# An eighth table read by one-hot products, one eviction per pick, and transposes issued a group ahead in a DLRM tower

## The chip, the cores and the metric

The kernel runs on one core of a Trainium2 chip. The metric is the device time of the core in microseconds (us), lower is better. A core has a matrix engine (TensorE, PE in the rows, its weight loads PEld), a vector engine (VectorE, DVE), a scalar engine (ScalarE, ACT), GpSimd (POOL) and SyncE (SP), which here only issues DMAs. Each engine runs its own instructions in order; between engines there are only semaphores.

## What is computed

For 512 samples, 26 rows of 128 numbers are looked up in 26 tables. All pairwise dot products of the 27 vectors of a sample (its dense vector and the 26 rows) go with the dense vector into a three-layer perceptron.

```python
e = jnp.stack([tbl_0[ids[:, 0]], ..., tbl_25[ids[:, 25]]], axis=1)      # 512 x 26 x 128
sd = jnp.einsum('bfd,bd->bf', e, dense)                                 # 26 dots
ss = jnp.einsum('bfd,bgd->bfg', e, e); pairs = ss[:, iu, ju]            # 325 dots
h = jnp.concatenate([dense, sd, pairs, dense], axis=1)                  # 512 x 607
h = jnp.maximum(h @ W_top1 + b_top1, 0.0)                               # 512
h = jnp.maximum(h @ W_top2 + b_top2, 0.0)                               # 256
y = h @ W_top3                                                          # 512 x 1
```

Eleven tables have 1250 rows, six 1000, the others 12500 and more.

## The kernel before

The batch is cut into four tiles of 128 samples, t = 0 to 3. The semaphore waits and the order of every engine's work are written out by hand.

**Hot tables, the pick stage.** Seven tables (`HOT`) are not gathered. Each is loaded whole, as 125 partitions of 8 rows (1000 rows) or 10 rows (1250 rows); one row per partition is a step. For table i, `spread_ids(i)` copies the 512 ids to all partitions with two matmuls (L342). ACT makes the rounded high part of the table (`round_table`, L757) and DVE the low part (`low_part`, L612). For each step a one-hot matrix of 512 columns says which sample wants the row: DVE makes most of them, two steps in an instruction (`one_hots`, L602), ACT makes the steps of `KS_ACT` in two instructions each (`distances`, L766, and L775). `pick(i)` sums high and low products of all steps in PSUM (L351), two 512-column matmuls a step. ACT reads the result out in two instructions (`read_picked`, L730 and L732): the first two tiles (`DIRECT = 2`) go straight into `vecs`, where the dot products are taken from, the other two into `early`, from which `place_early(2)` and `place_early(3)` (L746) bring them to `vecs` later. The one-hots lie in a ring of `HOT_STEPS` = 24 steps, the high and low parts in rings of 20.

**Cold tables.** The other 19 are joined in one tensor, and GpSimd gathers 128 rows with an indirect DMA (L323), 19 for each tile, 76 in all. They come in seven groups g = 0 to 6 a tile; `transposes(t, g)` turns a group on PE (L387, one 128-column matmul for each gather), `read_transposed(t, g)` copies it to `vecs` (DVE L590 for even g, ACT L737 for odd g). The rows of tiles 2 and 3 are gathered into the buffers of tiles 0 and 1, after their transposes.

**Dots and layers.** `gram(t, part)` takes the dots of 32 samples (L410, 8 matmuls; the trace counts 16). The last part of a tile is cut in two pieces, of the last tile in three. DVE and ACT copy them out (`read_sums`, L648 and L800). When the last part's sums are out, SP moves the tile's dots to the partitions that layer 1 wants with nine DMAs (`move_strips`, L275), and `layer_1(t)` (L438) waits for all of them (`s_dots[t]`). `layer_1_dense(t)` (L423) adds the dense part first. `layer_2(t)` and `layer_3(t)` follow. The last part of tile 3 is moved with matmuls (`move_last_part`, L451) and its other parts by five DMAs of SP and four of GpSimd (L333).

Of the kernel before, what the change touches and what calls it, by code (L numbers as in the profile page):

```python
# [11 lines left out]
P = 128  # L12
# [4 lines left out]
PITCH = 32  # L17
# [6 lines left out]
HOT = [5, 6, 7, 16, 19, 24, 2]  # L24
# [8 lines left out]
KS_ACT = [[4, 5, 6] if i in (1, 2, NHOT - 1) else [4, 5] for i in range(NHOT)]  # L33
# [6 lines left out]
HOT_STEPS, PART_STEPS, TABLE_RING = 24, 20, 3  # L40
EARLY = 1 + NHOT

DIRECT = 2
# [9 lines left out]
EXTRA_WIDTHS = [w for w in (1, 2, 4) if (len(COLD) - MAIN) & w]  # L53
assert EXTRA_WIDTHS[0] == 1
# [29 lines left out]
def build(nc, ins, out):  # L84
    with ExitStack() as ctx:
# [14 lines left out]
        dense_t = sb("dense_t", [P, TILES, P])  # L100
        early = sb("early", [P, EARLY, (TILES - DIRECT) * P])
# [48 lines left out]
        s_table = [sem(f"s_table{i}") for i in range(NHOT)]  # L150
        s_w1_dense = sem("s_w1_dense")
# [16 lines left out]
        s_picked = sem("s_picked")  # L168
        s_pick_read = sem("s_pick_read")
# [56 lines left out]
        def by_sample(x):  # L226


            return x.rearrange("d (h g s) -> d h s g", s=QUADS, g=PER_PART)
# [31 lines left out]
        def _(sp):  # L261
            def load_table(i):
# [3 lines left out]
                sp.dma_start(table[0:KP_A, i % TABLE_RING, 0:KTS[i]], whole[0:KP_A]).then_inc(s_table[i], 16)  # L266
# [37 lines left out]
        def _(pool):  # L304
            nc.gpsimd.memset(ident[:, :], 0.0).then_inc(s_zero, 1)
# [30 lines left out]
        def _(pe):  # L336
# [53 lines left out]
            def gram(t, part, piece=None):  # L390
                if part == 0:

                    if t < DIRECT:
                        pe.wait_ge(s_pick_read, NHOT)
                    else:
                        pe.wait_ge(s_early, t - DIRECT + 1)
                    pe.wait_ge(s_dve_read, uses_to(t, 0))
# [17 lines left out]
            def layer_1_dense(t):  # L415
# [5 lines left out]
                for bank, o0 in ((ps_h_act, OC1 // 2), (ps_h_dve, 0)):  # L421
                    for o in range(OC1 // 2):
                        pe.matmul(bank[:, o, :], w1_fold[:, (o0 + o) * P:(o0 + o + 1) * P], dense_t[:, t, :],  # L423
                                  start=(o == 0), stop=False, skip_group_check=True)
# [70 lines left out]
            pick(0)  # L495
            pick(1)
            transposes(0, 0)
            pick(2)
            transposes(0, 1)
            pick(3)  # L500
            transposes(0, 2)
            pick(4)
            transposes(0, 3)
            pick(5)
            transposes(0, 4)
            transposes(0, 5)
            pick(6)
            transposes(0, 6)
            transposes(1, 0)
            pe.wait_ge(s_pad, 2)  # L510
            pe.wait_ge(s_dense_read, 2)

            gram(0, 0)
            transposes(1, 1)
            gram(0, 1)
            transposes(1, 2)
            gram(0, 2)
            gram(0, 3, 0)
            gram(0, 3, 1)
            transposes(1, 3)  # L520
            gram(1, 0)
            transposes(1, 4)
            gram(1, 1)
            transposes(1, 5)
            transposes(1, 6)
            gram(1, 2)
            gram(1, 3, 0)
            gram(1, 3, 1)
            layer_1_dense(0)
            transposes(2, 0)  # L530
            layer_1(0)
            transposes(2, 1)
# [3 lines left out]
            transposes(2, 2)  # L536
            layer_1_dense(1)
            gram(2, 1)
            transposes(2, 3)
            transposes(2, 4)  # L540
            gram(2, 2)
            transposes(2, 5)
            gram(2, 3, 0)
            transposes(2, 6)
            gram(2, 3, 1)
            layer_1(1)
            transposes(3, 0)
            layer_2(1)
            layer_3(1)
            transposes(3, 1)  # L550
            layer_1_dense(2)
            gram(3, 0)
            layer_1(2)
            transposes(3, 2)
            layer_2(2)
            gram(3, 1)
            layer_3(2)
            transposes(3, 3)
            gram(3, 2)
# [14 lines left out]
        def _(dve):  # L574
# [40 lines left out]
            for i in range(NHOT):  # L615
# [5 lines left out]
                if i == 2:  # L621
                    dve.wait_ge(s_dense_tp, 1)
                    nc.vector.tensor_copy(dense_t[:, :, :], ps_dve[:, :, :]).then_inc(s_dense_read, 1)
                if i == 3:
                    read_transposed(0, 0)
                if i == 5:
# [285 lines left out]
```

## Time and profile before

| what | value |
|---|---|
| median of 3 runs | 119.66 us (117.87 to 120.6) |
| the profiled execution | 118.84 us |
| its span, first to last instruction | 116.9 us |
| PE busy | 104.5 us (89%) |
| POOL busy | 75.7 us (65%) |
| DVE busy | 63.5 us (54%) |
| ACT busy | 58.5 us (50%) |

The span lies 1.94 us below the execution's own time. Busy shares are averages over two stages: up to about 47 us the seven picks, with PE, DVE and ACT all full, and after it the dots and layers, with PE full and the other two half idle.

### The profile page before, as it was taken

To read this page: it belongs to the slowest core of one execution; us is meant where nothing else is said; L and a number is where in the kernel's file an instruction comes from. 1 tells how busy PE (TensorE), PEld (TensorE's weight loads), DVE (VectorE), ACT (ScalarE), POOL (GpSimd) and SP (SyncE) were. 2 spreads that over 40 slices of the span, in tenths; PEclk is the share of its full clock that TensorE was granted. 3 is DMA by queue.
4 is the path that set the end of the run, shared out by engine and by line. 5 is a ranking of instruction groups with operands and counts; after the bars stand their busy time and mean duration, and the time that the engine had idled before them with its cause. 6 is when DMAs were issued, how large, how long until landed. Compare 5 with 4: busy or idle time off the path is not lost.

```text
span 116.9 us, 1946 instructions
## 1 busy us (share of the span) xinstructions
PE 104.5 (89%) x696; PEld 90.7 (78%) x696; DVE 63.5 (54%) x140; ACT 58.5 (50%) x133; POOL 75.7 (65%) x88
## 2 busy tenths in 40 slices
PE   0679999999999688999999999978989997899991
PEld 0366676686868475999998998877979996799981
DVE  4779959997999990356746135225220343350030
ACT  4299549939976991255477235535212414340200
POOL 3777777677677767767767767767777775070000
PEclk9999999999999999999999999999999999999599
DMA  2997617362869822212233233112223112011000
GB/s 45 276 275 188 208 52 227 70 203 72 247 201 258 317 83 53 59 45 60 61 72 93 70 78 88 51 45 65 61 68 101 48 45 67 6 25 25 0 0 1
DMA packets 5709, 11.71 MB, mean 100 GB/s; under 512 B 2600, under 2 KB 3070, under 8 KB 5701
## 3 DMA queue, kind: packets, MB, share of 16 engines
q1 hardware_dynamic: 3141, 6.55, 18.9%
q0 software_dynamic: 2560, 5.05, 17.0%
q8 instruction: 5, 0.08, 0.3%
q14 instruction: 3, 0.02, 0.1%
HBM read 10.86 MB, written 0.00 MB: 93 GB/s over the span
## 4 chain that ended last, share of the span: by engine, by line
PE 79%; SPq 6%; DMA 5%; issue 3%; DVE 2%; ACT 2%
PE ps_gram L351 27%; PE ps_gram L410 19%; PE ps_h_bank L438 11%; SPq L275 5%; DMA dense<-in_r_dense_features 4%; PE ps_dve L387 3%; PE ps_h_bank L466 3%; PE ps_h_bank L423 3%; PE ps_act L387 3%; PE ps_gram L342 2%; DMA dots<-sums_even 2%; PE ps_dve L451 2%; PE ps_h_bank L478 1%; PE ps_h_bank L342 1%; PE ps_h_bank L469 1%
## 5 line engine op out<-in xcount | busy, mean ns | idle before, releaser
L323 POOL DMA_INDIRECT rows<-in_cold,cold_rows x72 | 68.8, 955 | 21.9 <-issue 21.3
L410 PE MATMUL ps_gram<-vecs 128*122 128x108 f32 x256 | 30.3, 271 | 2.3 <-ACT vecs L737 1.4
L410 PEld LDWEIGHTS ps_gram<-vecs 128*122 128x122 f32 x256 | 28.6, 187 | 3.5 <-ACT vecs L737 2.5
L351 PE MATMUL ps_gram<-one_hot,table_hi 125*128 125x512 f32 x58 | 24.7, 447 | 1.3 <-issue 1.3
L602 DVE TENSOR_TENSOR one_hot<-ps_gram,row_id 125x1024 fp32r<-125x1024 f32 (+1 forms) x22 | 25.0, 1138 | 0.7 <-PE ps_h_bank L342 0.7
L351 PE MATMUL ps_gram<-one_hot,table_lo 125*128 125x512 f32 x58 | 23.5, 426 | 0.0
L351 PEld LDWEIGHTS ps_gram<-one_hot,table_hi 125*128 125x128 f32 x58 | 11.7, 210 | 5.8 <-issue 3.0
L351 PEld LDWEIGHTS ps_gram<-one_hot,table_lo 125*128 125x128 f32 x58 | 12.0, 207 | 2.7
L438 PE MATMUL ps_h_bank<-dots,w_dots 128*128 128x128 f32 x96 | 13.2, 301 | 0.2 <-DMA dots<-sums_even 0.2
L612 DVE TENSOR_TENSOR table_lo<-table,table_hi 125x256 fp32r<-125x256 f32 x29 | 11.7, 412 | 2.9 <-ACT table_hi L757 2.8
L438 PEld LDWEIGHTS ps_h_bank<-dots,w_dots 128*128 128x128 f32 x96 | 12.7, 215 | 0.4 <-issue 0.4
L648 DVE COPY sums_even<-ps_gram 26x216 f32<-26x216 f32 (+1 forms) x20 | 6.5, 327 | 10.9 <-PE ps_gram L410 10.7
L590 DVE COPY vecs<-ps_dve 128x128 f32<-128x128 f32 (+2 forms) x20 | 8.1, 436 | 7.8 <-PE ps_dve L387 7.7
L800 ACT COPY sums_even<-ps_gram 26x216 f32<-26x216 f32 (+1 forms) x20 | 5.9, 296 | 11.1 <-PE ps_gram L410 10.9
L648 DVE COPY table<-ps_gram 26x216 f32<-26x216 f32 (+2 forms) x22 | 6.8, 310 | 7.6 <-PE ps_gram L410 7.2
L800 ACT COPY table<-ps_gram 26x216 f32<-26x216 f32 (+2 forms) x22 | 6.2, 283 | 9.1 <-PE ps_gram L410 8.9
L766 ACT ACTIVATE distance<-ps_h_bank,minus_row_id 125x512 f32<-125x512 f32 x17 | 10.6, 690 | 0.0
L757 ACT CAST table_hi<-table 125x1024 fp32r<-125x1024 f32 (+2 forms) x8 | 7.6, 966 | 5.1 <-PE ps_gram L351 2.9
L775 ACT ACTIVATE one_hot<-distance 125x512 fp32r<-125x512 f32 x17 | 9.7, 640 | 0.0
L737 ACT COPY vecs<-ps_act 128x512 f32<-128x512 f32 (+1 forms) x12 | 5.8, 480 | 6.2 <-PE ps_act L387 6.1
L656 DVE TENSOR_SCALAR h<-ps_h_bank,b 128x128 f32<-128x128 f32 x8 | 2.4, 346 | 11.5 <-PE ps_h_bank L438 11.5
L387 PE MATMUL ps_dve<-ident,rows 128*128 128x128 f32 x40 | 7.0, 274 | 0.5 <-DVE vecs L590 0.5
(63 smaller groups left out, 96.2 us busy)
## 6 DMA issues: line engine op xcount, KB each, us to landing
table<-in_tbl SPq DMA_DIRECT2D x6, 448.0 KB
rows<-in_cold,cold_rows POOLq DMA_INDIRECT x72, 2.5
w_dots<-in_w_dots SPq DMA_DIRECT2D x1, 768.0 KB, 5.6
table<-in_tbl SPq DMA_DIRECT2D x1, 560.0 KB
w_dense<-in_w_dense SPq DMA_DIRECT2D x1, 512.0 KB, 3.7
w<-in_W_top SPq DMA_DIRECT2D x1, 512.0 KB, 8.2
table<-in_tbl SPq DMA_DIRECT2D x6, 52.0 KB
dense<-in_r_dense_features SPq DMA_DIRECT2D x1, 256.0 KB, 4.2
```

Source lines behind the costliest of these rows:

```text
L323: pool.indirect_dma_start(out=rows[:, t % ROW_SETS, n, :], out_offset=None, in_=ins["cold"], in_offset=bass.IndirectOffsetOnAxis(ap=(cold_ ...
L351: return pe.matmul(ps_pick[:, i % 2, :], part[0:KP, (STEP_AT[i] + k) % PART_STEPS, :], one_hot[0:KP, (STEP_AT[i] + k) % HOT_STEPS, :], sta ...
L387: last = pe.transpose(bank[:, n - n0, :], rows[:, t % ROW_SETS, n, :], ident[:, :])
L410: last = pe.matmul(ps_gram[0:TAKEN, b0 + (g - g0) // PER_BANK, c0:c0 + COLS], vecs[:, t % 2, p0:p0 + QUADS, :].rearrange("d p f -> d (p f) ...
L438: last = pe.matmul(bank[:, o, :], w1_dots[:, j, (o0 + o) * P:(o0 + o + 1) * P], dots[:, t, :, j, :], start=False, stop=(j == STEPS - 1), s ...
L590: last = nc.vector.tensor_copy(dst, src)
L602: nc.vector.tensor_tensor(one_hot[0:KP, m:m + k1 - k0, :], ps_ids_dve[0:KP, i % 2, :].unsqueeze(1).to_broadcast(shape), row_id[0:KP, at + ...
L612: nc.vector.tensor_sub(table_lo[0:KP, n:n + PIECE], table[0:KP, i % TABLE_RING, k:k + PIECE], table_hi[0:KP, n:n + PIECE].bitcast(F32)).th ...
L648: last = nc.vector.tensor_copy(*own_sums(t, part, s, piece))
L766: nc.scalar.activation(distance[0:KP, n, :], ps_ids_act[0:KP, i % 2, :], ACT.Abs, bias=minus_row_id[0:KP, at + k:at + k + 1]).then_inc(s_d ...
L775: nc.scalar.activation(one_hot[0:KP, (STEP_AT[i] + k) % HOT_STEPS, :], distance[0:KP, n, :], ACT.Relu, bias=1.0, scale=-1.0).then_inc(s_ho ...
L800: last = nc.scalar.copy(*own_sums(t, part, s, piece))
```

## The change

- An eighth table (3, with 1250 rows) is picked, and the order of the tables is new. The steps go from 58 to 68, the gathers from 76 to 72 (18 a tile), `KS_ACT` gives ACT three steps of every table but tables 0 and 4, and the ring of one-hots has 22 steps.
- `read_picked` is one copy of 512 columns into `early`. `DIRECT` is gone, and the picked rows and the dense row of every tile are placed in `vecs` by copies from `early`: of tile 0 by ACT (parts 0 and 2) and DVE (parts 1 and 3), of tiles 1 to 3 by `place_early` on ACT. `dense_t` is now `early[:, 0]`.
- The larger piece of table 0's load (112 partitions) is issued by GpSimd, ahead of everything else there.
- On PE, picks 0 to 6 stand in a row with no transposes between them; most transposes stand one group further ahead of the gram that needs them, and the layers of a tile stand elsewhere among the grams.

```diff
-HOT = [5, 6, 7, 16, 19, 24, 2]
+HOT = [5, 6, 2, 7, 16, 3, 19, 24]
-KS_ACT = [[4, 5, 6] if i in (1, 2, NHOT - 1) else [4, 5] for i in range(NHOT)]
+KS_ACT = [[4, 5] if i in (0, 4) else [4, 5, 6] for i in range(NHOT)]
-HOT_STEPS, PART_STEPS, TABLE_RING = 24, 20, 3
+HOT_STEPS, PART_STEPS, TABLE_RING = 22, 20, 3
-DIRECT = 2
...
+        def placing(t, part):
+            p0 = part * PITCH
+            return (vecs[:, t % 2, p0:p0 + PITCH, 0:EARLY].rearrange("d (g s) f -> d f s g", s=QUADS),
+                    early[:, :, t * P + p0:t * P + p0 + PITCH].rearrange("d f (s g) -> d f s g", s=QUADS))
...
+            pool.dma_start(table[0:KP_A, 0, 0:KTS[0]], ins[f"tbl_{HOT[0]}"].rearrange("(p k) d -> p k d", k=KTS[0])[0:KP_A]
+                           ).then_inc(s_table_0_pool, 16)
...
             def gram(t, part, piece=None):
+                if t == 0:
+                    pe.wait_ge(s_placed_dve if part % 2 else s_placed_act, part // 2 + 1)
+                elif part == 0:
+                    pe.wait_ge(s_early, t)
...
             def read_picked(i):
                 act.wait_ge(s_picked, i + 1)
-                nc.scalar.copy(by_sample(vecs[:, :, :, 1 + i].rearrange("d t p -> d (t p)")),
-                               ps_pick[:, i % 2, 0:DIRECT * P].rearrange("d (h s g) -> d h s g", s=QUADS, g=PER_PART))
-                nc.scalar.copy(early[:, 1 + i, :], ps_pick[:, i % 2, DIRECT * P:]).then_inc(s_pick_read, 1)
+                nc.scalar.copy(early[:, 1 + i, :], ps_pick[:, i % 2, :]).then_inc(s_pick_read, 1)
...
# ACT, behind the picks
             read_picked(NHOT - 1)
+            act.wait_ge(s_dense_read, 1)
+            act.wait_ge(s_pick_read, NHOT)
+            nc.scalar.copy(*placing(0, 0)).then_inc(s_placed_act, 1)
+            read_transposed(0, 3)
+            nc.scalar.copy(*placing(0, 2)).then_inc(s_placed_act, 1)
...
# PE, tile 2's last grams and what follows
-            gram(2, 3, 1)
-            layer_1(1)
+            layer_2(1)
+            gram(2, 3, 1)
+            layer_3(1)
             transposes(3, 0)
-            layer_2(1)
-            layer_3(1)
             transposes(3, 1)
             layer_1_dense(2)
             gram(3, 0)
+            transposes(3, 2)
             layer_1(2)
-            transposes(3, 2)
+            gram(3, 1)
```

**On PE around layer 1 of tile 2.** From tile 2's last gram (L410 here, L419 in the changed file, waiting for `s_dve_read` and `s_act_read`) to the matmuls that wait for `s_dots2`, before:

```order
L410 MATMUL ps_gram<-vecs 122x108 x3
L438 MATMUL ps_h_bank<-dots,w1_dots 128x128 [waits s_dots1]
L438 MATMUL ps_h_bank<-dots,w1_dots 128x128 x11
...
L466 MATMUL ps_h_bank<-h1,w2 128x128 x3
L469 MATMUL ps_h_bank<-h1,w2 128x128 x2
L478 MATMUL ps_h_bank<-w3,h2 128x1 [waits s_h2_act_read,s_h2_dve_read]
...
L410 MATMUL ps_gram<-vecs 122x108 [waits s_sums_dve,s_act_read,s_sums_act,s_dve_read,s_early]
L410 MATMUL ps_gram<-vecs 122x108 x7
L438 MATMUL ps_h_bank<-dots,w1_dots 128x128 [waits s_dots2]
```

and in the changed kernel:

```order
L419 MATMUL ps_gram<-vecs 122x108 [waits s_dve_read,s_act_read]
L419 MATMUL ps_gram<-vecs 122x108 x3
L487 MATMUL ps_h_bank<-w3,h2 128x1 [waits s_h2_act_read,s_h2_dve_read]
L487 MATMUL ps_h_bank<-w3,h2 128x1
L393 MATMUL ps_dve<-ident,rows 128x128 [waits s_dve_read,s_rows1_0]
...
L432 MATMUL ps_h_bank<-early,w1_fold 128x128 x3
L419 MATMUL ps_gram<-vecs 122x108 [waits s_sums_dve,s_act_read,s_sums_act,s_dve_read,s_early]
L419 MATMUL ps_gram<-vecs 122x108 x7
L393 MATMUL ps_dve<-ident,rows 128x128 [waits s_dve_read,s_rows1_2]
L393 MATMUL ps_dve<-ident,rows 128x128 x3
L447 MATMUL ps_h_bank<-dots,w1_dots 128x128 [waits s_dots2]
```

Layers 1 and 2 of tile 1 have moved from behind tile 2's last gram to ahead of it; four transposes have come in between.

**On ACT ahead of tile 1's first gram.** L799 reads sums, L736 a transposed group, L744 is `place_early`; in the changed kernel:

```order
L799 COPY sums_even<-ps_gram 26x9x3x4 [waits s_gram]
L799 COPY sums_even<-ps_gram 26x9x3x4
L736 COPY vecs<-ps_act 128x32x16 [waits s_tp]
L744 COPY vecs<-early 128x9x4x8 x4
L799 COPY sums_even<-ps_gram 26x9x3x4 [waits s_gram]
```

and on PE at the same place:

```order
L393 MATMUL ps_act<-ident,rows 128x128 [waits s_act_read,s_rows1_1]
L393 MATMUL ps_act<-ident,rows 128x128 x3
L419 MATMUL ps_gram<-vecs 122x108 [waits s_dve_read,s_act_read,s_placed_dve]
L419 MATMUL ps_gram<-vecs 122x108 x3
L393 MATMUL ps_dve<-ident,rows 128x128 [waits s_dve_read,s_rows1_2]
L393 MATMUL ps_dve<-ident,rows 128x128 x3
L419 MATMUL ps_gram<-vecs 122x108 [waits s_sums_dve,s_act_read,s_sums_act,s_dve_read,s_early]
```

Before, tile 1's first gram waited for no `s_early`; its four copies are new here.

## Rows read from the trace of the kernel before

**Rows 1.** Page, part 4: the chain that ended last, shares by engine.

```profile
PE 79%; SPq 6%; DMA 5%; issue 3%; DVE 2%; ACT 2%
```

**Rows 2.** Chain in order of time (start us, us, what), one whole pick and its neighbours.

```profile
25.92 1.86 PE ps_gram L351 x8
...
28.43 2.06 PE ps_gram L351 x8
30.50 0.44 PE ps_dve L387 x4
...
40.01 1.30 issue
...
47.31 1.87 PE ps_gram L410 x16
```

**Rows 3.** Timeline of DVE (start us, us, engine, line, operation), table 6 of the picks.

```profile
40.98 1.21 DVE L602 TENSOR_TENSOR one_hot<-ps_gram,row_id 125x1024 fp32r<-125x1024 f32 x1
42.12 0.41 DVE L612 TENSOR_TENSOR table_lo<-table,table_hi 125x256 fp32r<-125x256 f32 x1
42.45 0.68 DVE L602 TENSOR_TENSOR one_hot<-ps_gram,row_id 125x512 fp32r<-125x512 f32 x1
43.05 0.41 DVE L612 TENSOR_TENSOR table_lo<-table,table_hi 125x256 fp32r<-125x256 f32 x1
```

**Rows 4.** Timeline of ACT, table 6 of the picks.

```profile
37.52 1.25 ACT L757 CAST table_hi<-table 125x1280 fp32r<-125x1280 f32 x1
38.67 1.84 ACT L766 ACTIVATE distance<-ps_h_bank,minus_row_id 125x512 f32<-125x512 f32 x3
40.39 0.61 ACT L730 COPY vecs<-ps_gram 128x256 f32<-128x256 f32 x1
...
41.08 1.70 ACT L775 ACTIVATE one_hot<-distance 125x512 fp32r<-125x512 f32 x3
```

**Rows 5.** Groups of instructions by form: busy us, mean ns, idle time before them and its releasers.

```profile
L410 PE MATMUL ps_gram<-vecs 128*122 128x108 f32 x256 | 30.3, 271 | 2.3 <-ACT vecs L737 1.4 <-DVE vecs L590 0.9
L478 PE MATMUL ps_h_bank<-w,h 128*128 128x1 f32 x16 | 2.2, 241 | 1.1 <-ACT h L813 1.1
L387 PE MATMUL ps_dve<-ident,rows 128*128 128x128 f32 x40 | 7.0, 274 | 0.5 <-DVE vecs L590 0.5
```

**Rows 6.** Chain, tile 0: last gram, landing of the last move, layer 1.

```profile
51.75 3.41 PE ps_gram L410 x32
...
61.92 2.21 DMA dots<-sums_even
...
64.27 2.92 PE ps_h_bank L438 x24
```

**Rows 7.** Chain, tile 2: last gram, layer 1 of tile 1, ..., layer 1 of tile 2, then tile 3.

```profile
80.08 1.07 PE ps_gram L410 x8
81.15 2.70 PE ps_h_bank L438 x24
...
90.53 2.74 PE ps_h_bank L438 x24
...
95.58 1.69 PE ps_gram L410 x16
...
103.77 0.91 PE ps_h_bank L423 x8
```

**Rows 8.** Timeline of SP's queue, the nine moves of tile 2.

```profile
81.76 6.86 SPq L275 DMA_DIRECT2D dots<-sums_even  x9
```

**Rows 9.** Timeline of ACT, `place_early(2)`.

```profile
60.08 1.97 ACT L746 COPY vecs<-early 128x256 f32<-128x256 f32 x4
```

**Rows 10.** A stretch of 1 us (columns: us, busy PE, PEld, DVE, ACT, POOL, granted clock, DMA share, GB/s), and the chain there.

```profile
108.00:109.00 1.00, 1.00 (x7) 1.00 (x7) 0.00 (x0) 0.00 (x0) 0.00 (x0) 0.50 0.00 0
...
107.49 4.34 PE ps_h_bank L438 x24
```

**Rows 11.** Timeline of POOL: the last gather.

```profile
97.47 0.94 POOL L323 DMA_INDIRECT rows<-in_cold,cold_rows x1 [0.30 <-issue]
```

## The prediction before the run

> **What bounds the kernel now.** I read three views in this order. First the chain that ended last, by engine: PE holds 79% of it, SP's queue 6% and DMA 5% [rows 1]. The reader is to see that time is won or lost on PE, or where PE waits for a transfer. Then the chain in order of time. In the pick stage it is PE without gaps: a whole 8-row pick with its `spread_ids` runs from 25.92 to 30.50, 4.58 us, at 0.235 us a product, and only once does PE stand still, 1.30 us at 40.01 [rows 2]. After the picks PE goes from 47.31 to 103.77 with short waits alone: 2.3 us ahead of grams for a late transposed group, 0.55 us twice ahead of layer 3, the second time behind 103.77 [rows 5]. Last the moves of the dots: in tile 0 the last gram ends at 51.75 + 3.41 = 55.16 and layer 1 starts at 64.27, which is 0.14 us behind the landing of the last move, at 61.92 + 2.21 [rows 6]. So **from a tile's last gram to its layer 1 there lie 9.11 us** of copies, nine issues in a row and a landing. In tile 2 the last gram ends at 80.08 + 1.07 = 81.15, the issues start at 81.76 and take 6.86 us [rows 8], and layer 1 starts at 90.53, 9.38 us behind the gram [rows 7]: PE had just enough work between. GpSimd starts the last gather at 97.47 without having waited for PE [rows 11]; it bounds nothing.
>
> **The change, part by part.** The sum is made against the profiled execution, 118.84 us, of which the span is 116.9 and 1.94 lies outside; the median of the runs is 0.8 us above it.
>
> *1. The eighth table.* Ten steps are 20 products of 0.235 us [rows 2]: +4.7 us on PE. `spread_ids` costs what a pick has above its 16 products, 4.58 - 3.76 = 0.8: +0.8. Ahead of the first gram stand 14 transposes (2 + 4 + 4 + 4) where there were 22, at 0.44 us for four [rows 2]: -0.9. The 1.30 us at 40.01 go: pick 6 waited there for `read_picked(4)`, which ACT reached late since it had waited for transposes among the picks, and those are gone. So goes a wait of 0.5 us ahead of tile 1's first group [rows 5]; with their restarts -1.9. New is a wait ahead of the first gram: behind the last pick ACT must copy 512 columns and place part 0, about 0.6 + 0.5 + 0.15, against 0.88 us of transposes on PE: +0.3 to 0.5. Sum: **+3.0 us** until the first gram.
>
> This holds if DVE and ACT keep up. DVE needs 1.14 us for two steps, 0.60 for one, 0.33 for a low part [rows 3]: 4.2 us for an 8-row table with three steps on ACT, 4.7 with two, 5.7 for ten rows, against 4.58 and 5.5 us of PE. ACT needs 0.9 or 1.15 for the rounding, 1.72 and about 1.6 for the three steps, and 0.5 for the read-out in place of 0.7 [rows 4]: 4.7 us a table, and PE's last two picks, without `spread_ids`, take only 3.8. Walked through from pick 2, with the round of a table waiting for the pick two before it, ACT's last one-hots come about 1.5 us ahead of their product, while DVE's of table 5 come at the very moment at which `spread_ids(7)` asks for them. The ring of 22 steps makes the last one-hots of a table wait for the pick two before it; that gives them a whole pick. Bounds: 0 to +2.5 us on top; I take 0.
>
> *2. Table 0 by way of GpSimd.* SP is rid of one issue of 0.76 us at most (6.86/9) [rows 8], GpSimd gets one of at most 1.25 us (0.94 + 0.30) [rows 11] ahead of the identity and of the gathers, and nothing here waits for gathers. No row shows such a load from GpSimd. Bounds -0.8 to +1.25; I take 0, since pick 0 starts only when the dense vectors have also come and been turned. The Trainium skill ("DMA: Bandwidth & Descriptors", Issuing engine by pattern) says that a DMA issued by sync or scalar is generally faster than one of GpSimd; by it the upper end is nearer, and the sum would rise by up to that 1.25.
>
> *3. Fewer gathers, more transposes behind the picks.* 58 transposes instead of 54 follow the first gram: **+0.4 us**. The four gathers less free 5 us of GpSimd, which bring nothing.
>
> *4. Transposes a group ahead.* From 47.31 to 103.77 PE has 56.5 us. By unit costs its work is 16 grams of 1.70 [rows 6], 54 transposes of 0.11, three layers 1 of 2.70, three dense parts of 0.91 [rows 7], and three layers 2 and 3 at two thirds of a layer 1 and 0.35: 50.3 us. Waits and restarts are thus 6.1 us, 2.85 of them waits in rows 5. Each transposed group now has a gram's time (1.70) to be read out in 0.6, and layer 3 a gram ahead of it. I take **-4.7 us**, and leave 1.4 for restarts that stay.
>
> *5. Placing tile 1.* `place_early(1)` is new and stands on ACT behind group 1 of tile 1, and tile 1's first gram waits for it. Its four copies take 1.97 us for 8 columns of `early` [rows 9], here there are 9, some 2.1; with the read-out of the group ahead of them 2.7, against the work that PE has at that place, half a gram and four transposes (0.85 + 0.44 = 1.3). **+1.5 us** with the restart (bounds +1.0 and +2.0). Behind it on ACT are the sums of tile 0's last piece, so tile 0's moves start 2 us later; their layer 1 has slipped back in PE's order to some 11.3 us behind the gram, where 9.1 + 2.0 are wanted, so nothing is added.
>
> *6. Layer 1 of tile 2.* This carries the forecast. Between tile 2's last gram and the `s_dots2` matmuls there stood layers 1 and 2 of tile 1, a gram and more, 9.4 us. Now there stand layer 3 (0.36), six transposes (0.66), a dense part (0.91), a gram (1.70) and four transposes (0.44): 4.1 us. The moves need the same copies, the same nine issues on SP, the same landing: 9.1 us [rows 6 to 8]. PE stands still for **+5.0 us**. What it is rid of there was already counted, as the layers of tile 1 now lie ahead of that gram; behind the wait all else queues, since PE runs in order, and no other engine has work to bring forward. What was done with the copies cannot shorten this: ACT and DVE read these sums at once in both kernels. Bounds +4.5 and +5.5.
>
> *7. The clock.* The one place where the granted clock falls is 108 to 109 us, at 0.50, the lower of its two levels (1.2 GHz), behind a stretch of small matmuls; layer 1 of tile 3 took 4.34 us there [rows 10], 2.70 elsewhere [rows 7]. No wait of PE before was longer than 1.30 us and none of those lowered it, so the trace does not tell what 5 us of standstill do. Bounds 0 and +3.3 (two such losses); I take **+1.6**, one layer 1 at the lower clock. The Trainium skill ("TensorE: Matmul & The Clock Gate", The HAM clock gate) says that the throttled level is the default, and that only activity releases it; by it the loss is sure and the sum ends at 125.6, not at the 124.0 of rival (a).
>
> Sum: 3.0 + 0.4 - 4.7 + 1.5 + 5.0 = 5.2, and 1.6 for the clock: 6.8. **118.84 + 6.8 = 125.6 us.**
>
> **The rivals.** (a) *The stall without the clock's fall*: 118.84 + 5.2 = 124.0. For it: PE is full on both sides of the wait. Against it: the wait is four times the longest of before. (b) *Not slower*: the moves of tile 2 are hidden. This needs a chain of at most about 4.1 us in place of 9.1, or work on PE that I count too short. Then the change gives 3.0 + 0.4 - 4.7 + 1.5 = 0.2: 119.0 us. For it speaks only that SP and the DMA engines are otherwise idle there; against it, that tile 0 measured 9.11 with nothing else in the way. It decides at a chain of some 4 us: every us above that is one of time, and past 6 the kernel is slower by over 2%. (c) *ACT or DVE becomes the bound of the picks*: up to 2.5 us on top, 128.1. For it: 4.7 us of ACT against 4.58 and 3.8 of PE, and DVE's zero slack at table 5. Against it: the walk above. (d) *The waits that a group ahead should take away come back elsewhere*, since the sums of a part now often stand behind a read-out on the same engine: 2 of the 4.7 us are taken back, 127.6.
>
> **How the numbers follow.** My forecast with the fall of the clock 0.5; (a) 0.23; (c) or (d) on top 0.15; (b) 0.09; the rest, an unforeseen gain, 0.03. The forecast's own spread is 1.5 us either way, from bounds 1, 2, 5 and 6. The range takes in (a) down to 122.6 and reaches to (c) at 128.0; outside are (b) and tails. About 2% (2.4 us) is what a measurement of this kernel can tell from no change, as its three runs lie 2.3% apart. Slower by over 2% is above 122.1: the first three cases but for their tails, 0.86. Within: (b) and those tails, 0.11. Faster: 0.03.
>
> **What the profile of the changed kernel would show.** First gram at 50 us (step 1); if it comes at 52 or later, with DVE or ACT full, (c) was right. No idle time ahead of transposes and few ahead of grams (step 4); one wait of 1.0 to 2.0 us ahead of tile 1's first gram, released by ACT's placing (5). One wait of 4.5 to 5.5 us ahead of the matmuls on tile 2's dots, released by a DMA (6), and a stretch at a granted clock of 0.5 behind it (7). Wrong would make me: no such wait, as then the time is near 119; or a first gram past 52.

## The result and the profile after

The changed kernel is slower: 125.62 us (median of 4 runs, 123.94 to 126.78) against 118.96 us, now the median of 4 runs of the kernel before (117.87 to 120.6). Some executions fall in a slower state, and the ratio is formed without them: it is 1.058, with a 95% interval of 1.041 to 1.075. Its profiled execution took 126.1 us, with a span of 124.2 where it was 116.9: 7.3 us more.

The waits of the changed kernel (engine, what it works on, line, what it waited for: us in total, times, longest):

```profile
PE ps_h_bank L447 <- DMA dots<-sums_even: 4.5, 1, 4.5
...
PE ps_dve L502 <- DMA dense<-in_r_dense_features: 1.8, 1, 1.8
...
PE ps_gram L419 <- ACT vecs L744: 1.5, 1, 1.5
...
PE ps_gram L419 <- DVE vecs L595: 1.1, 2, 0.6
```

L447 is layer 1's matmuls with the dots: one wait of 4.5 us, for the moves. L744 is `place_early`, once 1.5 us. Neither was there before [rows 5, 7]. L502 turns the dense vectors at the start, and L595 reads out transposed groups.

Its chain in order of time (start us, us, what), from start to end:

```profile
1.93 5.33 DMA dense<-in_r_dense_features
...
7.40 1.09 PE ps_dve L502 x4
...
50.99 1.93 PE ps_gram L419 x16
...
59.40 2.06 ACT vecs L744 x4
...
61.50 1.96 PE ps_gram L419 x16
...
88.71 0.85 PE ps_gram L419 x8
...
90.16 0.65 SPq L279
...
96.24 2.09 DMA dots<-sums_even
...
98.38 4.41 PE ps_h_bank L447 x24
...
112.49 0.91 PE ps_h_bank L432 x8
...
116.22 2.72 PE ps_h_bank L447 x24
```

The reader is to see three things. The chain leaves PE between 89.56, the end of tile 2's last gram, and 98.38 (PE itself still has work until about 93.9): it goes through DVE's copy, SP's nine issues and one landing, as it did for tile 0 before [rows 6]. Layer 1 of tile 2 behind that wait takes 4.41 us, and layer 1 of tile 3 in the tail 2.72: before it was the other way round, 2.74 and 4.34 [rows 7, 10]. And the stage of the grams starts at 50.99, not at 47.31 [rows 2].

The same in stretches (columns as in rows 10):

```profile
94.00:98.00 4.00, 0.00 (x0) 0.00 (x0) 0.90 (x2) 0.12 (x1) 1.88 (x2) 1.00 0.35 88
98.00:102.00 4.00, 3.62 (x19) 3.62 (x20) 0.00 (x0) 0.62 (x2) 0.00 (x0) 0.57 0.02 4
```

PE does nothing from 94 to 98, and the granted clock is 0.57 in the mean of the 4 us behind it. In the tail no stretch of the changed kernel is below 1.00.

That DVE kept up with the eighth table by a hair (0.2 us) shows at table 5, where `spread_ids(7)` asks for DVE's last one-hots. DVE's timeline, and PE's chain there:

```profile
36.83 0.69 DVE L607 TENSOR_TENSOR one_hot<-ps_gram,row_id 125x512 fp32r<-125x512 f32 x1
```

```profile
37.71 0.42 PE ps_gram L348
```

The one-hots end at 37.5, PE follows at 37.7 without a wait of its own.

### The profile page after: what moved, and what is told of

Same layout as the page of the kernel before. It is cut to its first block, busy times and chain, and to the rows that moved or that the text cites. A ratio compares the mean times of both kernels' runs of the same rounds, so it can differ in the third digit from the quotient of the medians.

```text
span 124.2 us, 2015 instructions
## 1 busy us (share of the span) xinstructions
PE 108.0 (87%) x714; PEld 93.8 (76%) x714; DVE 67.7 (54%) x149; ACT 68.4 (55%) x145; POOL 75.2 (61%) x85
## 4 chain that ended last, share of the span: by engine, by line
PE 79%; DMA 6%; SPq 5%; DVE 3%; ACT 2%; issue 2%
PE ps_gram L357 29%; PE ps_gram L419 20%; PE ps_h_bank L447 10%; SPq L279 5%; DMA dense<-in_r_dense_features 4%; PE ps_act L393 3%; PE ps_gram L348 2%; PE ps_h_bank L475 2%; PE ps_h_bank L432 2%; PE ps_dve L393 2%; PE ps_dve L460 2%; DMA dots<-sums_even 2%; ACT vecs L744 2%; PE ps_h_bank L348 1%; PE ps_h_bank L470 1%
## 5 line engine op out<-in xcount | busy, mean ns | idle before, releaser
L419 PE MATMUL ps_gram<-vecs 128*122 128x108 f32 x256 | 30.7, 271 | 3.2 <-ACT vecs L744 1.5
L419 PEld LDWEIGHTS ps_gram<-vecs 128*122 128x122 f32 x256 | 29.0, 187 | 4.1 <-ACT vecs L744 1.7
L607 DVE TENSOR_TENSOR one_hot<-ps_gram,row_id 125x1024 fp32r<-125x1024 f32 (+1 forms) x26 | 28.6, 1100 | 0.0
L357 PE MATMUL ps_gram<-one_hot,table_hi 125*128 125x512 f32 x68 | 28.3, 435 | 0.0
L357 PE MATMUL ps_gram<-one_hot,table_lo 125*128 125x512 f32 x68 | 27.2, 420 | 0.0
L357 PEld LDWEIGHTS ps_gram<-one_hot,table_hi 125*128 125x128 f32 x68 | 13.7, 205 | 5.4 <-issue 1.8
L447 PE MATMUL ps_h_bank<-dots,w_dots 128*128 128x128 f32 x96 | 13.0, 298 | 4.5 <-DMA dots<-sums_even 4.5
L447 PEld LDWEIGHTS ps_h_bank<-dots,w_dots 128*128 128x128 f32 x96 | 12.5, 213 | 4.8 <-DMA dots<-sums_even 4.8
L617 DVE TENSOR_TENSOR table_lo<-table,table_hi 125x256 fp32r<-125x256 f32 x34 | 13.7, 422 | 2.9 <-ACT table_hi L755 2.9
L764 ACT ACTIVATE distance<-ps_h_bank,minus_row_id 125x512 f32<-125x512 f32 x22 | 13.6, 687 | 0.0
L755 ACT CAST table_hi<-table 125x1024 fp32r<-125x1024 f32 (+4 forms) x10 | 9.0, 921 | 6.8 <-PE ps_gram L357 4.0
L773 ACT ACTIVATE one_hot<-distance 125x512 fp32r<-125x512 f32 x22 | 12.5, 650 | 0.0
L799 ACT COPY table<-ps_gram 26x216 f32<-26x216 f32 (+2 forms) x22 | 6.2, 283 | 11.0 <-PE ps_gram L419 9.9
L799 ACT COPY sums_even<-ps_gram 26x216 f32<-26x216 f32 (+1 forms) x20 | 5.9, 296 | 8.1 <-PE ps_gram L419 7.9
L339 POOL DMA_DIRECT2D dots<-table x4 | 2.1, 551 | 13.5 <-DVE table L646 13.5
L595 DVE COPY vecs<-ps_dve 128x128 f32<-128x128 f32 (+2 forms) x20 | 8.1, 435 | 3.9 <-PE ps_dve L393 3.7
L807 ACT ACTIVATE h<-ps_h_bank,b 128x128 f32<-128x128 f32 x8 | 2.5, 363 | 13.3 <-PE ps_h_bank L447 13.3
```

What stands on the lines that cost most here:

```text
L357: return pe.matmul(ps_pick[:, i % 2, :], part[0:KP, (STEP_AT[i] + k) % PART_STEPS, :], one_hot[0:KP, (STEP_AT[i] + k) % HOT_STEPS, :], sta ...
L419: last = pe.matmul(ps_gram[0:TAKEN, b0 + (g - g0) // PER_BANK, c0:c0 + COLS], vecs[:, t % 2, p0:p0 + QUADS, :].rearrange("d p f -> d (p f) ...
L447: last = pe.matmul(bank[:, o, :], w1_dots[:, j, (o0 + o) * P:(o0 + o + 1) * P], dots[:, t, :, j, :], start=False, stop=(j == STEPS - 1), s ...
L595: last = nc.vector.tensor_copy(dst, src)
L607: nc.vector.tensor_tensor(one_hot[0:KP, m:m + k1 - k0, :], ps_ids_dve[0:KP, i % 2, :].unsqueeze(1).to_broadcast(shape), row_id[0:KP, at + ...
L617: nc.vector.tensor_sub(table_lo[0:KP, n:n + PIECE], table[0:KP, i % TABLE_RING, k:k + PIECE], table_hi[0:KP, n:n + PIECE].bitcast(F32)).th ...
```

## The experiments

Eleven kernels ran, in three groups, each beside 7 runs of the kernel before. Its median was 118.61 us beside the first four (layers put back, filler, table 0 on SP, before with layers early), 116.95 beside the next four (the two placed by part and the two with seven tables) and 116.95 again beside the last three. The first gram starts anywhere from 48.9 to 51.1 us in kernels with the same picks, so I also compare what lies between it and the end of the span.

The traces show where the first gram's scatter comes from. In every execution the first products of PE stand 0.43 us apart, and later ones 0.235, though the granted clock reads 1.00 in all of these stretches. The full pace comes between 10 and 12.5 us in some executions and at about 16 us in the others, and the same second pick then takes 3.92 or 5.36 us. Chain of table 0 on SP, then of the changed kernel:

```profile
13.04 3.92 PE ps_gram L355 x16
```

```profile
13.05 5.36 PE ps_gram L357 x16
```

From the start of the dense vectors' transposes to the first gram the eight-table kernels need 41.9 to 42.4 us with the early pace and 43.6 to 43.7 with the late one; the two executions with the seven tables of the kernel before need 38.8 and 40.6. Why the pace comes early or late is not shown. The table says which it was.

| kernel | median us | full pace from, us | first gram | span | from first gram to the end |
|---|---|---|---|---|---|
| before | 118.96 | 16 | 47.31 | 116.9 | 69.6 |
| changed | 125.62 | 16 | 50.99 | 124.2 | 73.2 |
| layers put back | 119.74 | 11 | 49.25 | 119.1 | 69.9 |
| filler in the wait | 125.33 | 11 | 48.97 | 123.2 | 74.2 |
| table 0 on SP | 126.73 | 12 | 49.55 | 124.8 | 75.3 |
| before, layers early | 122.05 | 12 | 46.34 | 120.3 | 74.0 |
| placing by part | 125.79 | 16 | 51.07 | 124.1 | 73.0 |
| layers back, by part | 120.64 | 11 | 48.91 | 118.7 | 69.8 |
| layers back, seven tables | 120.05 | 16 | 45.60 | 118.2 | 72.6 |
| the same, by part | 119.73 | 16 | 45.62 | 118.6 | 73.0 |
| layers back, interleaved | 119.75 | 10 | 49.28 | 117.9 | 68.6 |
| the same, tail ahead | 119.49 | 16 | 50.76 | 117.9 | 67.1 |
| moves on two queues | 122.44 | 11 | 49.58 | 118.8 | 69.2 |

**Layers put back.** One part of the change undone, on PE (DVE and ACT in step):

```diff
-            layer_1(1)
             transposes(2, 6)
             gram(2, 3, 0)
-            layer_2(1)
             gram(2, 3, 1)
-            layer_3(1)
+            layer_1(1)
             transposes(3, 0)
+            layer_2(1)
+            layer_3(1)
             transposes(3, 1)
```

> The changed kernel with one part undone: layers 1 and 2 of tile 1 stand behind tile 2's last gram again, on PE, DVE and ACT, as in the kernel before. Theory (PE waits 4.5 us for the nine moves of tile 2 because the work between was moved ahead of them): the wait ahead of layer 1 of tile 2 falls from 4.5 to under 0.5 us, the fall of the clock behind it goes, and the time is 125.6 - 4.5 - 1.7 = 119.4 us, or 121 if the clock falls in the tail instead, as it did in the kernel before (1.6 us there). Rival (the waits go to another place, since the order as a whole is worse): the wait shrinks but the time stays above 123 us.

119.74 us, 5.9 less than the changed kernel. No wait for a DMA is left ahead of L447. Its chain:

```profile
93.63 2.68 PE ps_h_bank L447 x24
...
109.74 4.34 PE ps_h_bank L447 x24
```

Layer 1 of tile 2 runs at full clock, and the lower clock is in the tail. The first theory holds, with the tail's fall as its second branch had it. Of the 5.1 us between the two spans, 1.7 lie ahead of the first gram, where this execution had the early pace. Behind it 3.3 us are gained, not the 4.6 that the wait and the two clock terms make (4.5 + 1.7 - 1.6): 0.8 us of short waits are new, ahead of tile 2's last gram and of layer 3 of tile 1, and the rest is not measured apart.

**The order alone, in the kernel before.** The same move applied to the kernel before, the other way round; one group of transposes (2, 6) also moves ahead of half a gram, as in the changed kernel.

```diff
             transposes(2, 5)
+            layer_1(1)
-            gram(2, 3, 0)
             transposes(2, 6)
+            gram(2, 3, 0)
+            layer_2(1)
             gram(2, 3, 1)
-            layer_1(1)
+            layer_3(1)
             transposes(3, 0)
-            layer_2(1)
-            layer_3(1)
             transposes(3, 1)
```

> The kernel before with one part of the change alone: layers 1 and 2 of tile 1 stand ahead of tile 2's last gram, as in the changed kernel. Theory: between tile 2's last gram and its layer 1 there are 4.4 us of PE work in place of 9.4, the moves need 9.0, so PE waits some 4.6 us there; the layers that have moved cost nothing themselves. If the clock falls behind the wait and no longer in the tail, the time is 118.96 + 4.4 = 123.4; if it falls in both places 125.1. Rival (only with the eighth table is there a wait): within 1 us of 118.96.

122.05 us against 118.61: 3.4 us from this alone, and 1.35 below the forecast of 123.4. In the traces it is the 4.4 us that were forecast, from the first gram on (74.0 against 69.6); until it this execution had the early pace and the kernel before the late one. Its waits:

```profile
PE ps_h_bank L438 <- DMA dots<-sums_even: 4.6, 2, 4.5
```

and its chain:

```profile
93.22 5.10 PE ps_h_bank L438 x24
...
112.54 2.72 PE ps_h_bank L438 x24
```

The wait is the same 4.5 us with seven tables and the old transposes, so it belongs to the order of the layers and not to the eighth table. Behind it layer 1 takes 5.10 us, and the tail is spared in this execution, as in that of the changed kernel.

**Filler in the wait.**

```diff
             transposes(3, 2)
+            pe.wait_ge(s_act_read, uses_to(3, 1))
+            fill(18)
             layer_1(2)
```

> The changed kernel with 18 filler matmuls (identity by identity, thrown away) on PE right ahead of layer 1 of tile 2, some 3.9 us that lie inside its wait for the moves; nothing is moved. Theory (the standstill itself lowers the granted clock, and layer 1 pays for it): layer 1 of tile 2 still starts 8.8 us behind tile 2's last gram, its granted clock is 1.0 and it takes 2.7 us in place of 4.4, so the time is 1.7 us lower, 123.9, unless the clock falls in the tail instead (then 125.5). Rival (the clock falls whatever PE does there): 4.4 us as before, 125.6 us.

125.33 us. Its chain:

```profile
94.25 3.19 DMA dots<-sums_even
...
97.48 2.94 PE ps_h_bank L447 x24
...
113.86 4.34 PE ps_h_bank L447 x24
```

With PE busy in most of the wait the clock stays, and layer 1 of tile 2 takes 2.94 us. But it starts 9.9 us behind the gram, not 8.8: the last move needed 3.19 us from its issue in place of 2.09, for a reason that is not shown, and PE still stood for 1.6 us behind the filler. And the clock falls in the tail, 4.34 us, as in the kernel before. So it is the long standstill that lowers the clock behind it. In these two executions that costs nothing net: 1.7 us behind the wait, 1.6 spared later. Over the runs this is less sure. One of the filler's four had a mean granted clock of 1.0, with no fall anywhere, and took 122.7 us, where the three at 0.986 took 125.13 to 126.15.

**Table 0 on SP.** Both pieces of table 0 are issued by SP, as before.

```diff
-            pool.dma_start(table[0:KP_A, 0, 0:KTS[0]], ...).then_inc(s_table_0_pool, 16)
-                if i >= 1:
-                    sp.dma_start(table[0:KP_A, ...
+                sp.dma_start(table[0:KP_A, ...
```

> The changed kernel with table 0 loaded by SP alone, as in the kernel before. Theory (the piece on GpSimd makes the dense vectors land later, 7.27 against 6.56 us): the dense vectors land at 6.6 us, pick 0 starts 0.7 us earlier and all behind it too, 124.9 us. Rival (the later landing is chance or comes from the larger loads): no difference in the landing, 125.6 us.

The theory falls. The dense vectors' load is issued at 2.39 and lands 5.11 us later, at 7.50; so it does in the kernel before with the layers early (2.39, 5.05). With GpSimd's help it landed at 7.27 in the changed kernel and anywhere from 6.4 to 7.5 in the ten executions that have it, so the 6.56 of the kernel before was early by chance. GpSimd's issue does not delay the dense vectors. Table 0 itself comes later with it: its rounding on ACT starts at 5.4 to 5.9 us in the three executions with SP alone and at 5.9 to 6.6 in the ten with GpSimd. With the late pace nothing waits for that. The median of 126.73 has another reason. Both falls of the clock are in this one execution:

```profile
96.94 5.04 PE ps_h_bank L445 x24
...
115.66 4.06 PE ps_h_bank L445 x24
```

Three of its four runs had a mean granted clock of 0.96.

**Moves on two queues.** The order stays; SP issues five of tile 2's moves, ACT the other four.

```diff
-            move_strips(2, range(STRIPS))
+            move_strips(2, range(0, STRIPS, 2))
...
             read_transposed(3, 1)
+            act.wait_ge(s_sums_dve, chunks_to(2, PARTS - 1))
+            act.wait_ge(s_sums_act, chunks_to(2, PARTS - 1))
+            for q in range(1, STRIPS, 2):
+                dst, src = strip(2, q)
+                act.dma_start(dst, src).then_inc(s_dots[2], 16)
```

> The changed kernel, order kept, with four of the nine moves of tile 2 issued by ACT (behind its read of tile 3's group 1) and five by SP. Theory (PE's 4.5 us wait is the chain of nine issues one behind another on SP, 6.9 us, not the transfers): five issues on SP take 3.8 us, the four on ACT end some 4.6 us behind the gram, the last landing comes 6.7 us behind it in place of 8.8, the wait falls to 2.4 us, and the time from 125.6 to 123.5 us. Rival (the transfers themselves or their landing take the time): wait and time stay.

122.44 us. Its timelines of SP, ACT and PE:

```profile
88.77 3.79 SPq L279 DMA_DIRECT2D dots<-sums_even  x5
...
89.33 3.65 ACTq L848 DMA_DIRECT2D dots<-sums_even  x4
...
94.59 2.94 PE L447 MATMUL ps_h_bank<-dots,w_dots 128*128 128x128 f32 x24 [2.12 <-DMA dots<-sums_even]
```

Tile 2's last gram ends at 88.16, layer 1 starts 6.4 us behind it, and the wait falls from 4.5 to 2.1 us. The wait is mostly made by the issues one behind another. Behind 2.1 us of standstill the clock stayed, and in this execution it fell in the tail neither (2.72 us there). It is one execution, the fastest of four: the others took 121.84 to 123.32 us, with a mean granted clock of 0.972 or 0.986, so it fell somewhere in those.

**Placing by part.** Each of the four copies signals, each gram waits for its own.

```diff
-                elif part == 0:
-                    pe.wait_ge(s_early, t)
+                elif not piece:
+                    pe.wait_ge(s_early, PARTS * (t - 1) + part + 1)
...
-                    last = nc.scalar.copy(*placing(t, part))
-                last.then_inc(s_early, 1)
+                    nc.scalar.copy(*placing(t, part)).then_inc(s_early, 1)
```

> The changed kernel with each part of a tile's placing signalled by itself (one increment for each of the four copies, and each gram waits for its own part alone). Theory (tile 1's first gram waits 1.5 us since it needs all four copies although it reads one part): the wait falls to under 0.2 us and tile 2's last gram ends 1.5 us sooner, so 125.6 - 1.6 = 124.0 us. Rival (the sums that stand behind the copies on ACT hold the next gram instead): a wait of over 1 us moves to tile 1's second gram, 125.6 us.

125.79 us, nothing gained. PE's timeline:

```profile
70.86 2.92 PE L447 MATMUL ps_h_bank<-dots,w_dots 128*128 128x128 f32 x24 [1.21 <-DMA dots<-sums_even]
```

The wait of 1.5 us ahead of tile 1's first gram is gone, and one of 1.2 us has come at layer 1 of tile 0, whose moves wait for sums that ACT reads behind the four copies. The rival had the cause (sums behind the copies) but named the wrong place.

**Both together.** 

> Both mendings together: layers 1 and 2 of tile 1 behind tile 2's last gram, and the placing signalled by part. If the two waits are independent: 119.7 - 1.5 = 118.2 us, about the 118.6 of the kernel before. If taking away the placing wait only lengthens another one (moves of tile 0, or the sums): 119.7 us.

120.64 us, from the first gram 69.8 us against 69.9 with the layers put back alone: the same 1.2 us wait at layer 1 of tile 0. The second case holds.

**Interleaved.** ACT places part 0, reads the sums, then places the other parts.

```diff
-            place_early(1)
+            place_early(1, (0,))
             read_sums(0, 3, 1)
+            place_early(1, (1, 2, 3))
```

> Layers put back, placing signalled by part, and on ACT the sums of tile 0's last piece read between the placing of tile 1's part 0 and of its other parts. Theory (placing by part gained nothing because those sums still stood behind all four copies, so that the moves of tile 0 landed 1.2 us after PE wanted its layer 1): both waits are gone, no idle time over 0.3 us between the first gram and layer 1 of tile 0 but for the group ahead of tile 1, and the time is 1.2 us below the kernel with placing by part alone, 119.4 us. Rival (the nine moves are late for another reason, their issue): the wait of 1.2 us at layer 1 of tile 0 stays, 120.6 us.

Both waits are gone, and from the first gram to the end it takes 68.6 us in place of 69.8. That is the 1.2 us; the median, 119.75, is 0.9 lower, but the runs of the two kernels overlap (118.15 to 119.98 and 119.4 to 121.06), so the traces carry this and not the medians.

**Tail ahead.** Tile 3's last three transposed groups one group further ahead.

```diff
             transposes(3, 3)
+            transposes(3, 4)
             layer_2(2)
+            transposes(3, 5)
             gram(3, 2)
             layer_3(2)
-            transposes(3, 4)
-            transposes(3, 5)
-            gram(3, 3, 0)
             transposes(3, 6)
+            gram(3, 3, 0)
```

> The same, and in tile 3 the last three transposed groups also stand a group further ahead, with DVE and ACT reading them ahead of the sums. Theory (the 1.1 us of waits ahead of tile 3's last grams come from the read-out standing behind the sums of part 2): these waits are gone and the time is 1.3 us lower again, 118.1 us; against the 117 to 118.6 us of the kernel before that is the same. Rival (the moves of tile 3 then bound the end, since layer 1 of tile 3 comes sooner): the wait goes to layer 1 of tile 3 and the time stays at 119.4 us.

From the first gram to the end 67.1 us, 1.5 less: the waits of 0.7 and 0.4 us ahead of tile 3's last grams and their restarts are gone, and layer 1 of tile 3 waits for nothing. The median stays above the 118.1 us that were forecast. This execution had the late pace, and the first gram started 1.5 us later, so the span is the same, and the medians (119.49 and 119.75) cannot tell. Against the kernel before, which had the late pace too, this version is 2.5 us quicker behind the first gram and 3.4 us slower until it, and its median of 119.49 us lies above the 116.95 beside it: it does not beat it.

**Seven tables.** Table 3 gathered again, with the layers put back and the rest of the changed kernel kept.

```diff
-HOT = [5, 6, 2, 7, 16, 3, 19, 24]
+HOT = [5, 6, 2, 7, 16, 19, 24]
-EXTRA_WIDTHS = [1, 1]
+EXTRA_WIDTHS = [1, 2]
```

> The kernel with the layers put back (119.7 us) and seven picked tables in place of eight: table 3 is gathered again, 76 gathers, 58 steps; all else of the change stays. Theory (an eighth table costs PE 20 products and one spread, 5.5 us less 0.4 of transposes, and what it takes from GpSimd bounds nothing): 119.7 - 5.1 = 114.6 us if PE is still the bound. Since PE would then reach tile 3's groups 5.5 us sooner while the last gather still starts at about 98, I expect waits for gathers of 1.5 to 3 us there: 116.5 us. Rival (the eighth table's cost is hidden in waits that PE has anyway): 119 us or more.

> The same with the placing signalled by part: seven tables, layers back. If PE were the bound, 1.5 us less than the seven-table kernel; if the gathers are, as I expect, the wait only moves into tile 3 and the time is the same within 0.5 us. Both below the 118.6 us of the kernel before.

120.05 and 119.73 us, where 116.5 and about the same were forecast, and hardly better than eight tables (120.64 with placing by part, beside them). Of the two kernels with placing by part and the layers back, the one with seven tables has its first gram 3.3 us sooner (45.62 against 48.91), although it had the late pace and the other the early one, and takes 3.2 us more from there (73.0 against 69.8). At the same late pace eight tables with placing by part have the first gram at 51.07, 5.4 us behind. The waits with seven tables and the layers back:

```profile
PE ps_dve L393 <- DMA rows<-in_cold,cold_rows: 2.2, 2, 1.6
...
PE ps_act L393 <- DMA rows<-in_cold,cold_rows: 1.4, 2, 0.7
```

Its last gather on GpSimd's timeline, and that of the kernel with eight tables, layers back and placing by part:

```profile
101.00 0.94 POOL L329 DMA_INDIRECT rows<-in_cold,cold_rows x1 [0.30 <-issue]
```

```profile
95.73 0.94 POOL L329 DMA_INDIRECT rows<-in_cold,cold_rows x1 [0.30 <-issue]
```

PE waits for gathered rows, 3.6 us in four waits. My 116.5 us was too low, and the 119 us of the rival, which expected the eighth table's cost to be hidden in waits, was nearer. GpSimd was later than in the kernel before, 101.0 against 97.5 [rows 11]: the same 76 gathers took 0.99 us each where they took 0.95. The traces show where. Most gathers take 0.94 to 0.96 us, and those above 1.0 us, but for the first and one at 55.8 us, start while DVE is in `low_part`, whose two operands lie in SBUF. On GpSimd and DVE, seven tables and layers back:

```profile
34.83 1.49 POOL L329 DMA_INDIRECT rows<-in_cold,cold_rows x1 [0.30 <-issue]
```

```profile
34.75 0.76 DVE L617 TENSOR_TENSOR table_lo<-table,table_hi 125x256 fp32r<-125x256 f32 x2
```

Eleven gathers start so here and take 1.02 to 1.49 us; in the kernel before seven do, and take up to 1.17. That is 2.4 of the 3.5 us; the rest is a start 0.3 us later, behind the load of table 0, a first gather of 1.74 us in place of 1.14, and the one at 55.8 (1.19 us), which starts in another product of DVE with both operands in SBUF. That `low_part` holds the gathers up is read from where they lie; no run took it away. So the eighth table trades some 5 us of GpSimd for some 5 us of PE, and where PE is quick enough to meet the gathers the two are worth the same.

## Why the prediction was right, step by step

125.6 us was forecast and 125.62 measured, but not every term is as forecast. The sum was made on a profiled execution, and the profiled execution of the changed kernel took 126.1 us: the span grew by 7.3 us where the sum had 6.8:

| step | forecast | measured | from |
|---|---|---|---|
| start of PE's transposes of the dense vectors | 0 | +0.7 | 7.40 against 6.69, not a doing of the change |
| 1, eighth table, until the first gram | +3.0 | +3.0 | 50.99 - 7.40 against 47.31 - 6.69 |
| 3, four transposes more | +0.4 | not measured apart | taken as +0.4 in step 4 |
| 4, transposes a group ahead | -4.7 | -3.3 | what is left of 61.5 against 56.46 us |
| 5, placing tile 1 | +1.5 | +1.7 | the wait of 1.5 and its restart |
| 6, layer 1 of tile 2 | +5.0 | +4.5 | the wait |
| 7, clock | +1.6 | +0.1 | 4.41 - 2.70 behind the wait, 2.72 - 4.34 in the tail |
| the rest of the tail | 0 | +0.2 | 11.7 against 13.1 us, less the clock's part |

61.5 us is 112.49 - 50.99; of its 5.0 us more, 8.3 are steps 3, 5, 6 and the 1.7 of the clock, and the remainder, -3.3, is put down to the transposes.

**Step 6** was right in cause and place, and shown from both sides: the wait is gone with the layers put back, and it is there when they are moved in the kernel before. It was 4.5 us, not 5.0: the chain took 8.8 us, not 9.1, and PE's work beside it 4.3, not 4.1. Rival (b), moves that are hidden, is out.

**Step 1** held as a size. The +3.0 compares two executions with the late pace; the pair with the early one, table 0 on SP against the kernel before with the layers early, gives 41.9 against 38.8 us, about +3.1. DVE's zero slack at table 5 is as walked through. Rival (c) did not come here. It did in small in the five executions with both the early pace and GpSimd's load, where PE waited 0.2 to 1.2 us at about 21 us for one-hots of DVE. With the layers put back, its chain and its wait:

```profile
1.27 4.88 DMA table<-in_tbl
```

```profile
PE ps_gram L348 <- DVE one_hot L607: 0.8, 1, 0.8
```

**Step 4** was the one mis-sized term on PE: 3.3 in place of 4.7 us. The groups of tiles 1 and 2 brought what they should, but in tile 3 they do not stand a group ahead, and DVE reads the sums of part 2 before them. That is rival (d) in one place; the kernel with the tail ahead got 1.5 us of it back. Nor is all of the 3.3 the transposes' doing: the layers that moved ahead now fill short waits. In the kernel before they saved 0.8 us so, as it grew by 4.4 us where the wait and the clock make 5.2 (4.5 + 2.36 - 1.62), and putting them back in the changed kernel gave 1.3 us less than the wait and the clock make.

**Step 5** held as a size. But placing by part showed that its 1.5 us was not all to be had: behind it lay a second wait, for the moves of tile 0. I had put 11.3 us of PE work against 11.1 of moves there and called it nothing added; that margin was as thin as it looks, and used up once the first wait was gone.

**Step 7** missed as a term of this sum, which measured +0.1 in place of +1.6. The clock fell behind the wait, as forecast, with the price forecast. What I took for granted is that the fall in the tail would come again: in this execution it did not, so the two cancel. In two of the four runs of the changed kernel it may well have: their mean granted clock was 0.958 and 0.959, the latter the value of the execution with table 0 on SP whose trace has both falls. By the clock of the profiled execution rival (a) was nearer, and its 124.0 us missed by the other terms: 1.4 too much for step 4 and the 0.7 of the start, against 0.5 for step 6. The forecast's hit to 0.1 us is the luck of such terms cancelling; its sign, its size within a microsecond and its cause are not. The step also says that no wait of PE before was longer than 1.30 us. There was one at the start, ahead of the first products that stand 0.43 us apart:

```profile
PE ps_gram L342 <- ACT hot_ids_r L724: 3.5, 1, 3.5
```

The granted clock reads 1.00 there, but the spacing of the products does not, and it was the one sign in this trace that a longer standstill may come with slow products behind it. No run shows whether the wait causes them.

**Step 2** was taken as 0. For the dense vectors no cost shows against their scatter of 1.1 us; table 0 itself comes about half a microsecond later. In the late pace nothing waits for it; whether the waits of the early pace come from it or from the pace is not shown.

## What to carry to other kernels

When independent work stands between the producer of a slow transfer and its consumer on an in-order engine, it is the transfer's cover, and must be counted before any of it is moved: here 9.4 us of PE work covered a chain of 8.8 to 9.1, and moving it ahead of the gram cost 4.5 us. Count the chain as copies, issues one behind another and landing; if it must be shortened, share the issues between two queues. And after taking away one wait look at what is second there: the wait for the placing had another of 1.2 us behind it, and the gathers were second to the eighth table.

## What the runs showed of the hardware

The granted clock falls in two places. One is behind the long wait for the moves of tile 2, in all four profiled executions with a wait of 4.5 us (layer 1 took 4.41, 4.47, 5.04 and 5.10 us in place of 2.7). In the two where layer 1 took over 5 us it was down to 0.50 already within the wait, from 95 and from 91 us, and layer 1 ran wholly at the lower level. Behind waits of 1.6 us (filler) and 2.1 us (two queues) it did not fall. The other place is the tail, behind small matmuls with PE busy in all of the 3 us before: layer 1 of tile 3 took 4.34 us in the kernel before, with the layers put back and with the filler, and 3.88 to 4.34 in four more executions without the 4.5 us wait; it took 2.72 with seven tables and the layers back and with two queues.

Whether the tail's fall comes changes from run to run of one kernel; nothing here shows why. Of the 21 runs of the kernel before beside the experiments, ten had a mean granted clock of 1.0 and eleven 0.985 or 0.986. In the last group of seven the four at 1.0 took 115.94 to 116.95 us and the three at 0.985 took 117.66 to 119.18. One such fall is thus worth about 1.7 us. It is one source of this kernel's spread, and the early or late pace at the start, 1.2 to 1.9 us, is a second one that the mean granted clock does not show. Three of the four executions with a fall behind the long wait were spared the one in the tail, and the fourth, table 0 on SP, had both. But of the 16 runs of these four kernels seven had a mean clock of 0.959 or less, below the 0.972 that the longest single fall gave. So it is not shown that an earlier fall spares the tail.

A gather of 128 rows on GpSimd takes 0.94 us, but up to 1.50 us when it starts while DVE is in `low_part`, which reads two operands in SBUF. The gathers that start in DVE's one-hot instructions, of which one operand lies in PSUM, take 0.95 us at most. So it is in all 13 traces.

The same load of the dense vectors, issued at 2.39 us behind the same loads, landed after 4.17 us in one execution and after 5.05 and 5.11 in two others.
